# Dense items loaded and stored in pairs, rows of x fetched in place, attribute copies issued by ScalarE, in a graph layer with residual and layer norm

## What is computed

```python
edge_sum = segment_sum(edge_attr, src, num_segments=50000)
inputs = concatenate([x, edge_sum], axis=1)
h = elu(inputs @ W0 + b0)
h = elu(h @ W2 + b2)
y = x + (h @ W3 + b3)
out = (y - mean(y)) / sqrt(var(y) + 1e-5)
```

## Time and profile before

| | us |
|---|---|
| median of 3 runs | 602.74 (598.56 to 602.87) |
| profiled execution | 601.51 |
| its span, first to last instruction | 599.7 |
| TensorE / VectorE / ScalarE / GpSimd busy | 534.1 / 492.7 / 434.4 / 371.2 |

### The profile page before, as it was taken

How to read it: one execution, slowest core, us unless ns; L and a number is a source line. 1 busy time by engine, 2 the same in 40 slices (tenths; PEclk the granted TensorE clock), 3 DMA queues, 4 the chain that set the end, 5 groups by cost and what they waited for, 6 DMA issues and landing times.

```text
span 599.7 us, 11136 instructions
## 1 busy us (share of the span) xinstructions
PE 534.1 (89%) x2890; PEld 363.3 (61%) x2890; DVE 492.7 (82%) x1391; ACT 434.4 (72%) x1632; POOL 371.2 (62%) x310
## 2 busy tenths in 40 slices
PE   3899999779999999999899988788999999999980
PEld 1355555456566666677666655456676767777650
DVE  5988899788999989798888876667898888988961
ACT  2477775758888888786777774657788887888841
POOL 7766658466672778877887777785444333344306
PEclk9999999989999999999999999989999999999986
DMA  4567878677785777766666653344433444433101
GB/s 140 161 195 231 235 224 258 196 222 238 224 269 175 236 222 201 196 173 181 182 174 184 172 154 115 104 121 119 117 107 119 132 124 121 122 91 94 54 37 52
DMA packets 87766, 97.06 MB, mean 162 GB/s; under 512 B 26403, under 2 KB 56595, under 8 KB 87703
## 3 DMA queue, kind: packets, MB, share of 16 engines
q1 hardware_dynamic: 58807, 71.06, 37.8%
q0 software_dynamic: 28896, 25.29, 17.7%
HBM read 58.10 MB, written 45.04 MB: 172 GB/s over the span
## 4 chain that ended last, share of the span: by engine, by line
PE 57%; DVE 17%; issue 12%; ACT 6%; SPq 3%; another core or an unknown queue 1%; DMA 1%; POOL 1%; POOLq 0%; ACTq 0%; DVEq 0%
PE z_ps L568 13%; PE z_ps L569 13%; PE l_ps L524 11%; PE l_ps L556 11%; DVE e L862 4%; PE sum_ps L500 4%; ACT sq L638 3%; DVE h L865 3%; PE l_ps L535 3%; DVE o_sb L896 1%; PE turn_ps L549 1%; DMA x_sb<-x_items_dram 1%; SPq L323 1%; DVE net L759 1%
## 5 line engine op out<-in xcount | busy, mean ns | idle before, releaser
L638 ACT ACTIVATE sq<-z_ps 128x128 f32<-128x128 f32 (+1 forms) x493 | 129.8, 279 | 118.7 <-PE z_ps L569 68.1
L568 PE MATMUL z_ps<-center,xT 128*128 128x128 f32 (+1 forms) x986 | 194.5, 279 | 11.1 <-DVE h L865 9.6
L418 POOL DMA_INDIRECT out_dram<-pair_edge,target_i x100 | 120.5, 1205 | 122.4 <-issue 106.5
L569 PE MATMUL z_ps<-w3c,h 128*128 128x128 f32 (+1 forms) x986 | 191.1, 276 | 0.0
L568 PEld LDWEIGHTS z_ps<-center,xT 128*128 128x128 f32 (+1 forms) x986 | 153.5, 192 | 60.6 <-DVE h L865 30.6
L865 DVE SCALAR_TENSOR_TENSOR h<-l_ps,neg_bias,e 128x512 f32<-128x512 f32 (+1 forms) x214 | 159.1, 744 | 7.6
L397 POOL DMA_INDIRECT x_early<-in_x_dram,src_i x100 | 123.8, 1238 | 58.5 <-DMA pairs_dram<-x_early 28.6
L629 ACT ACTIVATE e<-l_ps,bias 128x512 f32<-128x512 f32 (+1 forms) x214 | 143.4, 670 | 13.4 <-PE l_ps L524 5.3
L407 POOL DMA_INDIRECT pair_edge<-pairs_dram,edge_i x100 | 124.0, 1240 | 42.6 <-issue 30.2
L569 PEld LDWEIGHTS z_ps<-w3c,h 128*128 128x128 f32 (+1 forms) x986 | 150.0, 192 | 0.0
L524 PE MATMUL l_ps<-xT,w0x 128*128 128x512 f32 (+1 forms) x248 | 131.7, 613 | 17.3 <-issue 12.5
(11 more groups left out here) (131 smaller groups left out, 372.7 us busy)
## 6 DMA issues: line engine op xcount, KB each, us to landing
x_sb<-x_items_dram SPq DMA_DIRECT2D x98, 256.0 KB
out_dram<-o_sb SPq DMA_DIRECT2D x98, 256.0 KB
pairs_dram<-x_early SPq DMA_DIRECT2D x25, 250.0 KB
keyB<-key_rows_dram SPq DMA_DIRECT2D x25, 250.0 KB
pairs_dram<-in_edge_attr_dram SPq DMA_DIRECT2D x24, 256.0 KB
x_early<-in_x_dram,src_i POOLq DMA_INDIRECT x100
pair_edge<-pairs_dram,edge_i POOLq DMA_INDIRECT x100
out_dram<-pair_edge,target_i POOLq DMA_INDIRECT x100
```

What stands on the lines that cost most here:

```text
L418: nc.gpsimd.indirect_dma_start(out=out[:, :], out_offset=bass.IndirectOffsetOnAxis(ap=target_i[0:EP, c:c + 1], axis=0), in_=pair_edge[0:EP ...
L568: T.matmul(z, xT[:, c % SLOTS, j * q:(j + 1) * q], center[:], start=True, stop=False)
L569: mm = T.matmul(z, h2[:, c % 2, j * q:(j + 1) * q], w3c[:], start=False, stop=True)
L638: t = A.activation(sq[0:q, j, :], z_ps[c % 2][0:q, j * P:(j + 1) * P], ACT.Square, scale=float(P) ** -0.5, accum_out=ssq[0:q, c % 2, j:j + 1])
```

## The change

- Dense items are loaded and stored in pairs. x_items is laid out so that one row of 4 KB in DRAM holds the part of a partition in both items of a pair (1,024 rows of x). x_sb and o_sb have three slots of pairs in place of four slots of items. A load is issued in the iteration of an even item, two pairs ahead (before three items), a store in that of an odd item, four steps on, and the pair before it is confirmed then. dense_out counts pairs, and dense_need is (key >> 10) + 2, at most 49.
- `fetch_x` writes the rows of x to pair_edge, where the gathers later put the sorted pairs. x_early and the waits for x_paired between fetches are gone; each group has a semaphore of its own, and the gathers wait for all copies as before. `pair_x(g)` moves from step 2 + 3g/2 to step 2 + 7g/6 (rounded down).
- `pair_attr` is issued by ScalarE at the head of steps 2 to 26.

```diff
-    AHEAD = 3
+    AHEAD = 2
+    PAIR_BITS = 10
+    ND2 = ND // 2
+    PAIR_SLOTS = 3
-    PAIR_X = {2 + 3 * g // 2: g for g in range(NE)}
+    PAIR_X = {2 + 7 * g // 6: g for g in range(NE)}
-        x_early = sb("x_early", [P, SLOTS, J, P])
-        x_sb = sb("x_sb", [P, SLOTS, J * P])
+        x_sb = sb("x_sb", [P, PAIR_SLOTS, 2, J * P])
-        o_sb = sb("o_sb", [P, SLOTS, J * P])
+        o_sb = sb("o_sb", [P, PAIR_SLOTS, 2, J * P])
...
-            def load(d):
-                if d >= SLOTS:
-                    sp.wait_ge(xT_ready, DENSE_AT[d - SLOTS] + 1)
-                sp.dma_start(x_sb[:, d % SLOTS, :], x_items[d * P:(d + 1) * P, :]).then_inc(x_loaded[d % SLOTS], 16)
...
+            def load(n):
+
+                k = n % PAIR_SLOTS
+                if n >= PAIR_SLOTS:
+                    sp.wait_ge(xT_ready, DENSE_AT[2 * (n - PAIR_SLOTS) + 1] + 1)
+                sp.dma_start(x_sb[:, k, :, :], x_items[n * P:(n + 1) * P, :].rearrange("p (h f) -> p h f", h=2))\
+                    .then_inc(x_loaded[k], 16)
+
+            def store(n):
+                k = n % PAIR_SLOTS
+                sp.wait_ge(o_ready, DENSE_AT[2 * n + 1] + 1)
+                if n == ND2 - 1:
+
+                    sp.wait_ge(stored[(n - 1) % PAIR_SLOTS], 16 * ((n - 1) // PAIR_SLOTS + 1))
+                first = min(2 * ROWS * n, N - 2 * ROWS)
+                sp.dma_start(out[first:first + 2 * ROWS, :].rearrange("(p h j) f -> p h (j f)", p=P, h=2), o_sb[:, k, :, :])\
+                    .then_inc(stored[k], 16)
...
             def pair_x(g):
-                k = g % SLOTS
-                sp.wait_ge(x_fetched[k], 16 * J * (g // SLOTS + 1))
+                sp.wait_ge(x_fetched[g], 16 * J)
                 sp.dma_start(pairs.rearrange("(p c) f -> p c f", p=EP)[:, J * g:J * g + J, 0:P],
-                             x_early[0:EP, k, :, :]).then_inc(x_paired[k], 16)
-
-            def pair_attr(g):
...
-                if item_in(c) and is_dense(c) and ITEMS[c][1] + AHEAD < ND:
-                    load(ITEMS[c][1] + AHEAD)
-                if item_in(c - 4) and is_dense(c - 4):
-                    d = ITEMS[c - 4][1]
-                    store(d)
-                    if d >= 2:
-                        confirm(d - 2)
-                if c in PAIR_ATTR:
-                    pair_attr(PAIR_ATTR[c])
+                if item_in(c) and is_dense(c) and ITEMS[c][1] % 2 == 0 and ITEMS[c][1] // 2 + AHEAD < ND2:
+                    load(ITEMS[c][1] // 2 + AHEAD)
+                if item_in(c - 4) and is_dense(c - 4) and ITEMS[c - 4][1] % 2 == 1:
+                    n = ITEMS[c - 4][1] // 2
+                    store(n)
+                    if n >= 1:
+                        confirm(n - 1)
...
             def fetch_x(g):
-                k = g % SLOTS
-                at_least(pool, x_paired[k], 16 * (g // SLOTS))
-                for j in range(J):
+
+                for c in range(J * g, J * g + J):
                     nc.gpsimd.indirect_dma_start(
-                        out=x_early[0:EP, k, j, :], out_offset=None, in_=x[:, :],
-                        in_offset=bass.IndirectOffsetOnAxis(ap=src_i[0:EP, J * g + j:J * g + j + 1], axis=0),
-                    ).then_inc(x_fetched[k], 16)
+                        out=pair_edge[0:EP, c, 0:P], out_offset=None, in_=x[:, :],
+                        in_offset=bass.IndirectOffsetOnAxis(ap=src_i[0:EP, c:c + 1], axis=0),
+                    ).then_inc(x_fetched[g], 16)
...
+            def pair_attr(g):
+                last = min(E, ROWS * (g + 1))
+                act.dma_start(pairs[ROWS * g:last, P:2 * P], attr[ROWS * g:last, :]).then_inc(attr_paired, 16)
...
             for c in range(STEPS_END):
+                if c in PAIR_ATTR:
+                    pair_attr(PAIR_ATTR[c])
                 parts = []
...
-                link(V.tensor_scalar(dense_need[0:1, :], dense_need[0:1, :], ROW_BITS, None, ALU.logical_shift_right))
-                V.tensor_scalar(dense_need[0:1, :], dense_need[0:1, :], 2, ND, ALU.add, ALU.min).then_inc(ends_ready, 1)
+                link(V.tensor_scalar(dense_need[0:1, :], dense_need[0:1, :], PAIR_BITS, None, ALU.logical_shift_right))
+                V.tensor_scalar(dense_need[0:1, :], dense_need[0:1, :], 2, ND2, ALU.add, ALU.min).then_inc(ends_ready, 1)
```

More of the change, by code:

```diff
@@ L49, in gnn_resnorm @@
     WORD_ROWS = -(-E // P)
-    ROW_BITS = 9
-    assert ROWS == 1 << ROW_BITS
+    PAIR_BITS = 10
+    ND2 = ND // 2
+    PAIR_SLOTS = 3
+    assert ND % 2 == 0 and 2 * ROWS == 1 << PAIR_BITS
     SLOTS = 4
     SUM_SLOTS = 5
-    AHEAD = 3
+    AHEAD = 2
     DENSE_BETWEEN = 2
@@ L256, in gnn_resnorm @@
         keyB_loaded = [sem(f"keyB_loaded{k}") for k in range(SLOTS)]
-        x_fetched = [sem(f"x_fetched{k}") for k in range(SLOTS)]
-        x_paired = [sem(f"x_paired{k}") for k in range(SLOTS)]
+        x_fetched = [sem(f"x_fetched{g}") for g in range(NE)]
+        x_paired = sem("x_paired")
         attr_paired = sem("attr_paired")
@@ L261, in gnn_resnorm @@
         dense_out = sem("dense_out")
-        x_loaded = [sem(f"x_loaded{k}") for k in range(SLOTS)]
-        stored = [sem(f"stored{k}") for k in range(SLOTS)]
+        x_loaded = [sem(f"x_loaded{k}") for k in range(PAIR_SLOTS)]
+        stored = [sem(f"stored{k}") for k in range(PAIR_SLOTS)]
         scattered = sem("scattered")
@@ new lines, in store, with confirm @@
+            def store(n):
[6 more added lines that the diff above has]
+                    .then_inc(stored[k], 16)
+            def confirm(n):
+                sp.wait_ge(stored[n % PAIR_SLOTS], 16 * (n // PAIR_SLOTS + 1))
@@ L335, in confirm @@
                 sp.sem_inc(dense_out, 1)
             def pair_x(g):
-                k = g % SLOTS
-                sp.wait_ge(x_fetched[k], 16 * J * (g // SLOTS + 1))
+                sp.wait_ge(x_fetched[g], 16 * J)
                 sp.dma_start(pairs.rearrange("(p c) f -> p c f", p=EP)[:, J * g:J * g + J, 0:P],
-                             x_early[0:EP, k, :, :]).then_inc(x_paired[k], 16)
-            def pair_attr(g):
-                last = min(E, ROWS * (g + 1))
-                sp.dma_start(pairs[ROWS * g:last, P:2 * P], attr[ROWS * g:last, :]).then_inc(attr_paired, 16)
+                             pair_edge[0:EP, J * g:J * g + J, 0:P]).then_inc(x_paired, 16)
@@ L381, in _ @@
                     load_keys(SUMS[c] + SLOTS)
-            confirm(ND - 2)
-            confirm(ND - 1)
+            confirm(ND2 - 1)
         @block.gpsimd
@@ L425, in _ @@
                 fetch_x(g)
-            for k in range(SLOTS):
-                pool.wait_ge(x_paired[k], 16 * len(range(k, NE, SLOTS)))
+            pool.wait_ge(x_paired, 16 * NE)
             pool.wait_ge(attr_paired, 16 * NE)
@@ L439, in _ @@
                 scatter_out(g)
-            pool.wait_ge(dense_out, ND)
+            pool.wait_ge(dense_out, ND2)
             pool.wait_ge(o_ready, LAST + 1)
@@ L889, in normalise @@
                 if kind == "dense":
-                    at_least(dve, stored[n % SLOTS], 16 * (n // SLOTS))
-                    rows_out = o_sb[:, n % SLOTS, :].rearrange("p (j f) -> p j f", j=J)
+                    at_least(dve, stored[n // 2 % PAIR_SLOTS], 16 * (n // 2 // PAIR_SLOTS))
+                    rows_out = o_sb[:, n // 2 % PAIR_SLOTS, n % 2, :].rearrange("p (j f) -> p j f", j=J)
                 elif kind == "edge":
@@ L959 @@
     x_in = inputs['x']
-    starts = [min(c * J * P, x_in.shape[0] - J * P) for c in range(-(-x_in.shape[0] // (J * P)))]
-    turned = _np.concatenate([x_in[n:n + J * P].reshape(P, J, P).transpose(2, 1, 0).reshape(P, J * P) for n in starts])
+    two = 2 * J * P
+    starts = [min(n, x_in.shape[0] - two) for n in range(0, x_in.shape[0], two)]
+    turned = _np.concatenate([x_in[n:n + two].reshape(P, 2 * J, P).transpose(2, 1, 0).reshape(P, two) for n in starts])
     arrays["x_items_dram"] = _np.ascontiguousarray(turned)
```

9 lines of the change are left out of this document (3 added, 6 removed).

## The result

The changed kernel takes 623.72 us (median of 4 runs, 622.34 to 626.33) against 602.81 for the kernel before beside it (598.56 to 605.21): ratio 1.0362, 95% interval 1.0314 to 1.0411. I had said 597.5 and 584 to 609: slower by 21 us where I forecast 5 less. Its profiled execution took 626.33 us, its span is 624.5, 24.8 longer than before's.

The account below looks back on a forecast made before the run. TensorE was busy 89% of the span; the largest loss was seen in slow edge-item stretches beside unbroken GpSimd work. 601.5 - 5 - 2 + 0 + 2.5 = 597.0, raised by half of 1.2 to 597.5 us; range 584 to 609.

Parts of the forecast that it names:

- fetches in place: Rows of x fetched into pair_edge without pauses, moving GpSimd's unbroken work out of the edge stage: -5 us, bounds +3 and -24.
- the shift: Gathers begin near 163 us in place of 196.28, 33 us earlier; by itself this gives nothing.
- The slow stretch: Edge items beside unbroken gathers and scatters, from 240 us: loss of 24.1 us, to be 19.5 after the change.
- Rival 3: Steps 2 to 26: ScalarE's attribute copy issues lie on the path, 0.50 us each, 12.5 in all, 610 us; chance 0.15.
- Copies on SyncE: Copies of x rows at earlier steps, SyncE standing at x_fetched: 0, up to +3 us if word_rows is late.
- Pairs: Dense loads and stores by pairs, gaining at the end of the sort: -2 us, bounds +1 and -6.
- Rival 4: Load target might be cut into 2 KB halves, shown by packet counts; time stays 597.5 us; chance within the forecast's 0.45.
- The tail: Release of group 23's scatter waits for the last pair's store, 2.5 us later, fully on the path: +2.5 us.

Follow-up runs that it names:

- g4: The changed kernel with the old copy steps and no pauses between fetches: 631.51 us, 1.0383 of the kernel before.
- g3: The changed kernel with the old waits between fetches and the old copy steps: 606.43 us, 1.0024 of the kernel before.
- g1: The changed kernel itself once more, beside the kernel before at 603.9 us: 621.71 us, 1.0281.
- e4: The kernel before with only the fetches in place, their pauses gone and the copies at the new steps: 619.06 us, 1.0298.
- h1: The kernel before with gathers and scatters reordered and spaced by waits on a count of normalised items: 582.80 us, 0.9629.
- e1: The kernel before with only the attribute copies issued by ScalarE at the head of steps 2 to 26: 603.12 us, 1.0005.
- f1: The kernel before with only the copies of x rows to pairs at the new steps: 575.42 us, 1.0178.
- f4: The changed kernel with the old waits between fetches and old copy steps, beside the kernel before at 566.71 us: 569.39 us, 1.0056.
- f3: The kernel before with only the place that the fetches write changed, old waits and copy steps kept: 569.69 us, 1.0030.

## Why the prediction was wrong

**The term that failed is the one for fetches in place**, -5 with the bounds +3 and -24. I held that the shift itself gives nothing and that the lost pauses cost at most 28.6 us at 0.103 a us. The measured cost of taking the pauses away is 25 us between g4 and g3, which differ in nothing else (631.51 to 606.43). With the new copy steps besides it is 15 (g1 against g3) and 17 (e4 against before). By item 16 the traces are 23 to 30 us late (g1 and e4 at 130.8, the changed kernel at 138.4, before at 107.9). The step of the prediction that failed: I priced the 28.6 us of pauses as so much more GpSimd work, but the loss isn't paid on the pauses. Once they are gone the run of 150 us is unbroken, and the steps beside it are long, from item 0 to the end of the sort. My own rates on the whole run give 150 x 0.103 = 15 us (gathers) to 150 x 0.213 = 32 us (scatters), a range that holds what was measured. That is worked out afterwards, and that such a rate carries over from edge items to the sort is not shown. I had tied the loss to unbroken work beside *edge* items. The earlier trace rows bore that out in part, with 4.0 us an item from 160 to 240 us, where the gathers run unbroken beside dense items from 196 us on. What I had no row for is an unbroken run beside the sort: the pauses kept the kernel before from showing one.

**The slow stretch.** Its size was right: 24 us of loss priced, 21.8 won back by h1. What I predicted of it was wrong in part. The gathers did not move (196.1), so the shift that the -5 was worked out from never came. The stretch did shrink. I read it so: the items come 30 us later, so more of the unbroken gathers lie beside dense items, and the scatters catch up sooner, their first pause ending at 406.5 in place of 414.83; 8 us come back. That is read from the trace of one execution, not isolated, and it is luck as far as the prediction goes.

**Rival 3** named the right place, the early steps, and the right sign, by the wrong cause. The gap behind ScalarE's own issue is there in the trace, 7.2 us in 17 steps, 0.42 each, and e1 gives 1.0005 for the same issues beside the pauses, as the cover that I took from the earlier trace rows would have it. The rule I cited from the Trainium skill, "DMA: Bandwidth & Descriptors", section "Issuing engines are not separate DMA queues", says that another issuer saves only the time of issue. e1 agrees so far as the move won nothing either: the 25 issues of 0.50 us were not on the path on SyncE's side.

**Copies on SyncE**, 0 with +3 if word_rows is late: late it was, by 4.5 us, where the early steps are short enough (f1, 575.42 against 566.71, +9, of which the late words are about half). With steps of 6 to 7 us it has cover: g4 with the old steps is no faster than g1. The term was under-sized, and its condition had been named. In the changed kernel's own trace no item waits for a load of x.

**Pairs**, -2: no run shows it. f4 and f3, which differ by pairs (with their later release in the tail) and ScalarE's copies, give 569.39 and 569.69. In their traces item 121 stands at 548.5 and 547.9, so the pairs won nothing up to there; g3, with pairs, is not below the kernel before. Both comparisons would hide 2 us in the medians. Rival 4 falls too, packets went from 87,766 to 73,653 on the page.

**The tail**, +2.5: the scatter of group 23 starts 2.1 us behind the last dense normalisation where it had started 0.4 us ahead of it in the earlier trace rows:

```profile
607.85 1.19 POOL L413 DMA_INDIRECT out_dram<-pair_edge,target_i  x1 [18.22 <-SPq L339]
```

```profile
605.75 0.69 DVE L896 TENSOR_TENSOR o_sb<-z_ps,rstd 128x512 f32<-128x512 f32 x1
```

(GpSimd, then VectorE, in order of time.) 2.1 + 0.4 = 2.5, as worked out.

The sum with the terms as this trace has them: 601.5 + 30 (early steps) - 8 (slow stretch) + 2.5 (tail) = 626.0, for 626.33. It closes because the terms are read from the same execution; what the experiments isolate is the first.

## What to carry to other kernels

A wait that looks like a loss on an idle engine may be what lets the others run: before taking pauses out of a long run of GpSimd's indirect DMAs, look in the trace for other unbroken runs of the same instructions and read what the items cost beside each, and what work stood beside it (here no more than 4.0 us an item beside plain dense items, up to 0.213 us per us beside edge items). Bound the price by such rates on the whole run, not on the pauses. Where a rate is above zero, spacing the run (a wait on a count of finished items each four DMAs) is a small change to try. Here spacing and reordering the gathers and scatters gave 3.7% on the kernel before, on a chip where it takes 606 us; no run shows what it gives on the others. Put a run of the unchanged kernel beside each set of runs, since chips differ.

## What the runs showed of the hardware

- On chips where the kernel before takes about 603 us, a run of indirect DMAs of 1.21 us with gaps of 0.30 beside the sort goes with long waits of ScalarE before the squares, 2.7 us each (40.9 us in 15, 22 to 140 us), though at the one followed above (98.00 us) every engine that the program waits for there had finished. The starts behind them lie mostly 0.14 to 0.28 or 0.86 to 1.02 us behind a fetch's start. With gaps of 2.5 to 6.5 us every few groups (28.6 us in 7) such waits are 5.4 us in 2. Beside plain dense items, 198 to 238 us, the same run has none. The releaser is one that the profile can't name, so that TensorE's signal comes late is my reading; it is not shown. Which half of the DMA's work does it, the issue or the traffic, stayed open.
- The Trainium skill, "SBUF — State Buffer", section "SBUF: two separate sides", has one place on the engines' side where GpSimd can hold up another compute engine, the port pair that it shares with VectorE, and says that TensorE and ScalarE never wait on anyone there. The trace doesn't speak against that: VectorE's first layer takes 679 and 681 ns, ScalarE's squares 0.28 us each after the long waits, and what grew is the wait ahead of them. So this rule about ports doesn't explain the loss.
- The same kernel takes 602.5 to 605.7 us on some chips and 565.9 to 566.7 on others (medians of 12 to 25 runs), at nearly the same granted clock (0.982 in the profiles of before and of f1). None of the faster chips' traces has an unnamed wait before the squares. The difference of 37 us is larger than the changed kernel's whole loss; h1, on a chip of 605.66 us, wins back 23 of it.
